# Attention on one Trainium2 core: four weighted value rows summed by accumulating transposes on TensorE instead of by additions on GpSimd and VectorE

## What is computed

```python
qh = _split_heads(layernorm(x) @ Wq.T)
k, v = jnp.split(ctx @ Wkv.T, 2, axis=-1)
gather = seg_id[:, :, None] - jnp.arange(4)          # four rows per token
k_sel, v_sel = kh[b, :, clip(gather)], vh[b, :, clip(gather)]
scores = jnp.einsum('bhqd,bhqkd->bhqk', qh, k_sel) * HDIM ** -0.5   # masked where gather < 0
probs = jax.nn.softmax(scores, axis=-1)
out = jnp.einsum('bhqk,bhqkd->bhqd', probs, v_sel)   # the sum over the four weighted value rows
x = x + out.reshape(b, lq, 512) @ Wo.T
x = x + ffn(layernorm(x))                            # quantised gate, up and down projections
```

## Time and profile before

| | |
|---|---|
| median of 3 runs | 2349.54 us (2347.63 to 2350.33) |
| span of the profiled execution, first to last instruction | 2347.3 us |
| what lies around the span | not shown by the profile; the runs' median is 2.2 us above it |
| busy: PE, DVE, ACT, POOL | 86%, 73%, 60%, 29% of the span |
| mean granted TensorE clock | 0.947 of full speed |
| attention stage | about 61 us (first product) to 634 us |
| DMA in the whole span | 634.6 MB, mean 270 GB/s |

### The profile page before, as it was taken

How to read it: one execution, slowest core, us unless ns; L and a number is a source line. 1 busy time by engine, 2 the same in 40 slices (tenths; PEclk the granted TensorE clock), 3 DMA queues, 4 the chain that set the end, 5 groups by cost and what they waited for, 6 DMA issues and landing times.

```text
span 2347.3 us, 25386 instructions
## 1 busy us (share of the span) xinstructions
PE 2020.4 (86%) x9524; PEld 945.0 (40%) x9524; DVE 1715.7 (73%) x1387; ACT 1398.2 (60%) x1599; POOL 670.6 (29%) x662
## 2 busy tenths in 40 slices
PE   5888888888599999999999999999000699999998
PEld 2444444444244444444444444444000344444443
DVE  8799999999634534532499998999899644577641
ACT  4678887887422322322499996676899633366530
POOL 2599999998300000000121110222111000000000
PEclk9999999999799999999999999999555899999999
DMA  7789999998346656743699995787998755555541
GB/s 297 283 314 337 348 337 346 335 350 316 126 181 226 225 207 223 259 148 144 242 378 390 378 369 209 264 320 293 401 419 327 291 229 208 205 201 232 233 152 72
DMA packets 131162, 634.60 MB, mean 270 GB/s; under 512 B 12256, under 2 KB 12768, under 8 KB 91104
## 3 DMA queue, kind: packets, MB, share of 16 engines
q1 hardware_dynamic: 85888, 316.81, 37.0%
q0 software_dynamic: 45152, 316.16, 34.6%
HBM read 430.69 MB, written 202.24 MB: 270 GB/s over the span
## 4 chain that ended last, share of the span: by engine, by line
PE 64%; issue 3%; DVE 3%; ACT 2%; POOL 0%; DVEq 0%; ACTq 0%; POOLq 0%
PE fd_pp L1777 42%; PE fd_pp L1791 21%; ACT ff_ring L1720 1%; DVE ff_sig L1575 1%; DVE ff_h_parts L1559 1%; DVE ff_sq L1497 1%; ACT ff_sig L1707 0%; DVE ff_sq L1566 0%; DVE kept_gate L1568 0%; DVE ff_gin L1510 0%; DVE ff_hq L1549 0%; ACT ff_hq L1632 0%; ACT ff_ring L1746 0%; ACT ff_sig L1736 0%; DVE kept_o_peak L1575 0%
## 5 line engine op out<-in xcount | busy, mean ns | idle before, releaser
L1791 PE MATMUL fd_pp<-ff_down,kept_gate 128*128 128x512 f16 x1536 | 458.9, 381 | 193.1 <-DVE ff_up L1616 193.1
L1777 PE MATMUL fd_pp<-ff_h_parts,kept_gate 128*128 128x512 f16 x2304 | 499.6, 380 | 14.3 <-DVE ff_h_parts L1415 14.3
L1777 PE MATMUL fd_pp<-ff_h_parts,ff_up 128*128 128x512 f16 x2304 | 497.4, 379 | 0.0
L1639 ACT ACTIVATE ff_raw<-fd_pp 128x1024 f32<-128x1024 f32 x192 | 194.3, 1017 | 396.5 <-PE fd_pp L1777 396.5
L1777 PEld LDWEIGHTS fd_pp<-ff_h_parts,kept_gate 128*128 128x128 f16 x2304 | 225.9, 98 | 287.9 <-DVE ff_h_parts L1415 14.7
L1777 PEld LDWEIGHTS fd_pp<-ff_h_parts,ff_up 128*128 128x128 f16 x2304 | 225.4, 98 | 271.8
L1420 DVE TENSOR_REDUCE kept_gate_peak<-ff_raw 128x1 f32<-128x2048 f32 x48 | 109.7, 2285 | 292.9 <-ACT ff_raw L1639 292.9
L1791 PEld LDWEIGHTS fd_pp<-ff_down,kept_gate 128*128 128x128 f16 x1536 | 150.6, 98 | 375.9 <-issue 195.8
L1791 PE MATMUL fd_pp<-ff_down,ff_up 128*128 128x512 f16 x768 | 292.2, 380 | 0.0
L1746 ACT ACTIVATE ff_ring<-ff_hq,kept_g 128x2048 int16<-128x2048 f32 x48 | 96.0, 1999 | 191.1 <-DVE ff_hq L1549 189.7
L790 PE MATMUL at_psO<-kept_wo,at_ahi 128*128 128x512 f16 x512 | 155.5, 386 | 36.2 <-ACT at_alo L277 31.6
(11 more groups left out here) (239 smaller groups left out, 3454.9 us busy)
## 6 DMA issues: line engine op xcount, KB each, us to landing
ff_raw<-up_scratch SPq DMA_DIRECT2D x66, 1024.0 KB, 8.5
gate_scratch<-ff_raw POOLq DMA_DIRECT2D x48, 1024.0 KB, 9.1
ff_gin<-gate_scratch SPq DMA_DIRECT2D x48, 1024.0 KB, 8.7
up_scratch<-ff_raw POOLq DMA_DIRECT2D x48, 1024.0 KB, 7.7
ff_gin<-gate_integers SPq DMA_DIRECT2D x73, 512.0 KB, 5.8
gate_integers<-ff_ring POOLq DMA_DIRECT2D x43, 512.0 KB, 8.7
ff_up<-up_scratch SPq DMA_DIRECT2D x21, 1024.0 KB, 9.5
kept_xs<-in_x SPq DMA_DIRECT2D x32, 512.0 KB, 14.6
```

The lines of the kernel that those rows point to most:

```text
L1639: nc.scalar.activation(raw[:, n % UNITS, h * 2 * BLK:(h + 1) * 2 * BLK], pp[(2 * n + h) % 4][:, :, :].rearrange("p a t -> p (a t)"), ACT.C ...
L1777: mm = nc.tensor.matmul(pp[k % 4][:, h, :], wt[w][:, c, f:f + P], a[:, b % 2, :, c, :], start=(q == 0), stop=(q == len(todo) - 1))
L1791: mm = nc.tensor.matmul(pp[k % 8 // 2][:, k % 2, :], a[b % 2][:, f, t * P:(t + 1) * P], wt[w][:, f, :], start=(q == 0 and i == 0), stop=(q ...
```

## The change

The additions go. VectorE's `weigh` multiplies value row 0 only (512 elements instead of 1536); GpSimd multiplies rows 1 to 3 in one instruction (`weigh_upper`, 1536 elements), for the last two tiles too. `turn_a` issues 16 transposes instead of 4: for each of the four rows of `kv` its four 128x128 blocks, all into psA, with `start` only on the first and `stop` only on the last, so that PSUM adds the four transposed rows. It waits for `pv` and `last` of its tile instead of for `att`. `att` gives its room to an unused tensor of the same size. `sum_last` and the semaphores `half` and `att` are gone.

GpSimd's order in a slot changes: first gather_next(2s-3), then weigh_upper(2s-2) and (2s-1), then norms(s), then gather_next(2s-2). gather_next(t) now waits for `aT` of tile t, the end of its transposes, since these read the gathered rows themselves. SP's wait for the 60th tile is for `aT` too.

```diff
-        att, hn = (r.sb(n, [P, 2, D], F32) for n in ("att", "hn"))
+        r.sb("room", [P, 2, D], F32)
+        hn = r.sb("hn", [P, 2, D], F32)
...
-                        sp.wait_ge(m["att"], KR * (NT // KR) - KR + 6 if NT % KR == 0 else NT - NT % KR)
+                        sp.wait_ge(m["aT"], KR * (NT // KR) - KR + 6 if NT % KR == 0 else NT - NT % KR)
...
                 def weigh(t):
-                    values = kv[:, t % KR, 0:W - 1, D:2 * D].rearrange("p w (h e) -> p w h e", h=H)
-                    nc.vector.tensor_tensor(values, values, pr[:, t % 2, 0:W - 1].unsqueeze(3).to_broadcast([P, W - 1, H, HD]),
+                    values = kv[:, t % KR, 0, D:2 * D].rearrange("p (h e) -> p h e", h=H)
+                    nc.vector.tensor_tensor(values, values, pr[:, t % 2, 0].unsqueeze(2).to_broadcast([P, H, HD]),
                                             ALU.mult).then_inc(m["pv"], 1)
...
-                def sum_last(t):
...
                         if s_ == NP - 1:
-                            sum_last(a)
                             residual(a - 2)
                         weigh(a + 1)
-                        if s_ == NP - 1:
-                            sum_last(a + 1)
...
-                def weigh_fourth(t):
-                    last = kv[:, t % KR, W - 1, D:2 * D].rearrange("p (h e) -> p h e", h=H)
+                def weigh_upper(t):
+                    upper = kv[:, t % KR, 1:4, D:2 * D].rearrange("p w (h e) -> p w h e", h=H)
                     pool.wait_ge(rows_in[t % KR], 16 * (t // KR + 1))
                     pool.wait_ge(m["pr"], t // 2 + 1)
                     if t < LAST - 1:
                         pool.wait_ge(m["pv"], t // 2 * 2 + 2)
-                    nc.gpsimd.tensor_tensor(last, last, pr[:, t % 2, W - 1].unsqueeze(2).to_broadcast([P, H, HD]),
+                    nc.gpsimd.tensor_tensor(upper, upper, pr[:, t % 2, 1:4].unsqueeze(3).to_broadcast([P, 3, H, HD]),
                                             ALU.mult).then_inc(m["last"], 1)
-                def add_up(t):
...
                 def gather_next(t):
-                    pool.wait_ge(m["att"], t + 1)
-                    gather(t + KR)
+                    if tile(t) and t + KR < NT:
+                        pool.wait_ge(m["aT"], t + 1)
+                        gather(t + KR)
...
                     if s_ == NP:
-                        weigh_fourth(LAST - 1)
-                        weigh_fourth(LAST)
+                        weigh_upper(LAST - 1)
+                        weigh_upper(LAST)
                     if pair(s_ - 1) and s_ < NP:
-                        add_up(2 * s_ - 2)
-                        add_up(2 * s_ - 1)
-                        gather_next(2 * s_ - 2)
-                        gather_next(2 * s_ - 1)
+                        gather_next(2 * s_ - 3)
+                        weigh_upper(2 * s_ - 2)
+                        weigh_upper(2 * s_ - 1)
                     if s_ > 0 and (pair(s_ - 3) or pair(s_ + 3)):
                         norms(s_)
+                    if pair(s_ - 1) and s_ < NP:
+                        gather_next(2 * s_ - 2)
...
                 def turn_a(t):
-                    pe.wait_ge(m["att"], t + 1)
+                    pe.wait_ge(m["pv"], t + 1)
+                    pe.wait_ge(m["last"], t + 1)
                     need(pe, m["alo"], t)
-                    turn(psA, att[:, t % 2, :]).then_inc(m["aT"], 1)
+                    for j in range(W):
+                        for c in range(DC):
+                            mm = nc.tensor.matmul(psA[:, c, :], kv[:, t % KR, j, D + c * P:D + (c + 1) * P], ident[:, :],
+                                                  is_transpose=True, start=(j == 0 and c == 0), stop=(j == W - 1 and c == DC - 1),
+                                                  skip_group_check=True)
+                    mm.then_inc(m["aT"], 1)
```

More of the change, by code:

```diff
@@ L187, in opening @@
         rows_in = [r.sem(f"rows_in{i}") for i in range(KR)]
-        m = r.sems("xn xT xhi xrest xlo q prod raw sc top ds ex tot inv pr pv last half att aT ahi arest alo o x1 "
+        m = r.sems("xn xT xhi xrest xlo q prod raw sc top ds ex tot inv pr pv last aT ahi arest alo o x1 "
                    "nmean ssq ssq_v stat aggr sqe root rstd norm x_nmean x_ssq hn hT hT_sb peak h_red h_all reduced")
```

## The result

The changed kernel takes 2365.61 us (median, 2364.72 to 2366.49), the kernel before 2349.11 (2347.63 to 2350.33) beside it: a ratio of 1.0073, 95% interval 1.0061 to 1.0085, 16.5 us slower. The profiled execution spans 2364.4 us, 17.1 more than before.

What follows compares the result with a forecast made beforehand. VectorE set the pace before, TensorE's chain after, at 17.51 us per slot. Terms 6.7 + 13.5 + 1.3 - 4.6 = +16.9 us on the profiled 2347.3, plus 2.2 to the median: 2366; own range 2356 to 2376, widened to 2353 to 2384.

Steps and rivals of the forecast that it cites:

- Transposes: TensorE's turn_a: 12 more transposes per tile at 0.11 us each, adding ones included, 2.64 us more work per slot.
- Rival 2: Transposes that add in PSUM cost more: at 0.215 us each, 3.4 us per slot, +105, 2471 us; chance 0.08.
- A slot: One pass over s_, two token tiles, in attention: 17.51 us by TensorE's chain against 16.95, 0.56 more.
- Both round trips: TensorE's waits for ScalarE's copies, before turn_a(2s-3)'s subtraction and the slot's last projection: 0.6 and 0.4 us per slot.
- The four early slots: Attention slots from 103.41 to 166.53: 63.12 us before, 69.9 by TensorE's chain, +6.7.
- The 24 slots: Steady attention slots to 573.25: 24 x 17.51 = 420.2 us for 406.72, +13.5.
- The end: Behind the last full attention slot: VectorE's sums go, turn_a(63) costs 1.3 more, TensorE idles less; together -4.6 us.
- two -3: At attention's end: about -3 us from VectorE's sums going, -3 from TensorE's idle times and 1.2 GHz matmuls going.
- The hold: VectorE's scaling, blocked on the port shared with GpSimd from 7 to 9.6 us into the slot; doesn't decide.
- Rival 3: GpSimd, its lock or the late gather holds VectorE: 18 to 18.9 us per slot, 2380 to 2408 us; chance 0.10.
- Gathers: Issued later in attention slots, needed 14.7 (odd tile) and 17 us after issue; odd can be 2 late; nothing added.
- rival 1: TensorE's round trips get covered by other work: a slot costs 16.48 us, 2336 us in all; chance 0.07.

Runs made afterwards that it cites:

- e9: Changed kernel with every value row starting anew in PSUM, same 16 transposes, so only row 3 is left: 2366.22 us (1.0075).
- e3: Changed kernel with value row 0 added twice, 20 transposes a tile instead of 16: 2393.43 us (1.0192).
- e6: Changed kernel with TensorE issuing the next slot's turn_x ahead of project_out(2s-2), result unchanged: 2353.17 us (1.002).
- e5: Changed kernel with GpSimd weighing row 1 only, rows 2 and 3 left unweighted, 16 transposes kept: 2366.09 us (1.0074).
- e4: Changed kernel with the weighing split as before: VectorE rows 0 to 2, GpSimd row 3, TensorE still sums by 16 transposes: 2365.96 us (1.0073).
- e7: Changed kernel with GpSimd also adding rows 2 and 3 to rows 0 and 1, TensorE summing by 8 transposes: 2388.94 us (1.0176).
- e11: As e10, with ScalarE's low copy ahead of take_xn(2s+5) and TensorE's next turn_x ahead of project_out(2s-2): 2338.72 us (0.996).
- e10: Changed kernel with VectorE weighing rows 0 and 1, GpSimd weighing rows 2 and 3 and adding them to 0 and 1, 8 transposes: 2372.86 us (1.0102).

## Why the prediction was right

**The forecast** was 2366 us, by TensorE's chain; 2365.61 came, and the profiled spans differ by 17.1 where the sum had 16.9. Term by term:

- *Transposes*: 0.11 each, adding ones too; 0.109 measured, and e9 shows that adding is free. Rival 2 falls.
- *A slot*: 17.51 forecast, 17.54 measured. What bounds it is shown by e3 (every further transpose on the path) and e6 (0.43 back from one round trip). Both round trips were where the chain had put them. By the starts they cost 0.63 and 0.42 us, 0.6 and 0.4 forecast; by the profile's modelled ends TensorE is idle for 0.47 ahead of 527.66 and 0.25 ahead of 539.57.
- *The four early slots*: 69.9 forecast; 103.92 to 173.90 is 69.98. They began 0.5 later than before, which the sum did not have. *The 24 slots*: +13.5 forecast, 420.88 - 406.72 = +14.2. *The last full slot*: +1.3, measured 594.78 to the turn at 612.31, 17.53 against 16.24.
- *The end*: -4.6 forecast. From the last slot's turn to the last turn_h it took 41.13 us before (589.49 to 630.62) and takes 36.25 (612.31 to 648.56), so -4.9. The f16 pairs of the projections there take 0.59 to 0.61 us, the 2.4 GHz level, as against the 1.06 of the earlier trace rows. The waits of 4.66 and 2.22 us are gone; the longest ahead of a projection is 0.96. Between the five turns of att the times change by -4.90, +0.66, -0.56 and -1.40, and behind the last one by +1.32, the 1.3 forecast for turn_a(63). The forecast's two -3 can't be told apart in this.
- *What the sum left out*: the measured terms add up to 17.9 (0.5 + 6.9 + 14.2 + 1.3 - 4.9). The span grew by 17.1, because what lies behind the last turn_h took 1715.8 us instead of 1716.7. The sum had nothing for this and no run explains it, so that 16.9 came within 0.2 of 17.1 is partly luck; the slot, 17.51 for 17.54, is not.
- *GpSimd*: 3.0 taken, 2.79 measured, the multiplication's own slope rather than three times the short one. It cost nothing, as e5 shows. *VectorE*: 2.1 us less work, worth nothing, as e4 shows.
- *The hold*: forecast from 7 us into the slot until the end of GpSimd's second multiplication at 9.6; measured 6.4 to 9.3 (531.05 to 533.89, the slot starting at 524.63), off the path. Rival 3 falls for this kernel. Its mechanism is real all the same: in e7 it decides. The Trainium skill's SBUF — State Buffer (Terms), by which the loser is blocked for the full instruction, agrees with both.
- *Gathers*: landing in 8.6 to 11.7 us now, median 10.4, so the odd one's 14.7 us were ample.

**What missed**: VectorE was to show about 85% busy with waits. It shows 97%, because a held instruction counts as busy; e5's 83% is what it does without the hold. And rival 1, that the round trips might be covered, doesn't hold for this order, but e6 shows that one of them can be.

In short, the additions went to an engine that had 3.1 us of waits per slot. It took 2.64 us more work, and its waits fell to 1.06 (17.54 less 16.48 of work), by VectorE's 1.17 us and some 0.9 of the round trips. The 0.6 that found no room is what each slot is longer.

## What to carry to other kernels

When two engines stand near each other, compare what the relieved one gives with what the other must take, and chain the other's instructions start to start through its round trips: busy shares (99% and 87%) said that there was room, the chain said that there was not. Then look at the order before the work: with a quarter of the transposes left to a short addition and two operations moved, the same idea is 0.8% faster than the kernel before (whose own order was not changed in any run). And before an engine's instruction is made longer, ask which short operations of the engine that shares its port come while it runs, and whether their end is on the path: 2.5 us of hold cost nothing in one kernel and decided in another.

## What the runs showed of the hardware

A VectorE operation with two SBUF inputs that comes while GpSimd computes is shown as one long busy instruction: 128 elements took 0.35 us alone and 2.84 held, and ended some 0.15 us behind GpSimd's instruction. TensorE's granted clock was 1.00 in the slots of e11 and of the changed kernel, while in e10 it was 0.91 in every fourth or fifth slot: in the one at 472.16 the f16 pairs from 487.90 take 1.06 instead of 0.59 us, the 1.2 GHz level, after waits of 0.86 and 1.06 us ahead of 485.31 and 487.20. f32 transposes that add in PSUM run at 0.109 us each, the pace of those that overwrite, 16 in a row. Two gathers of 2 MB landed in 8.6 to 11.7 us where they are issued 5.5 and 12 us apart in turn, and in 8.1 to 16.7 where they were issued in pairs.
